# The first three q tiles copied out by ScalarE and multiplied by GpSimd, with one rope moved up and zeros in the first lap

## The reference, cut to what matters

```python
q_hk  = (hidden_q @ Wq.T).reshape(Bv, Sv, H, K)
q_big = jnp.einsum('bshk,hkq->bshq', q_hk, w_kc_q)          # 192 columns a head
q_big = _apply_rope(q_big, sin_q, cos_q)                    # x * cos + rotate_half(x) * sin
q_r   = jnp.einsum('bshq,hqr->bhsr', q_big, W_qr)           # 64 columns a head
scores = jnp.einsum('bhsr,bhlr->bhsl', q_r, k_r)
attn  = jax.nn.softmax(scores, axis=-1)
ctx   = attn @ kv_r, then through w_kc_kv and Wo, added to x with a gate
```

## Time and profile before

| | |
|---|---|
| median of 3 runs | 547.29 us (544.44, 547.29, 547.99) |
| the profiled execution, its time | 546.06 us |
| its span, first to last instruction | 543.9 us |
| hand-over (end of the first mixture to the first scores) | about 206 to 227 us |
| laps | about 227 to 435 us |
| mean granted clock of TensorE | 0.959 of full speed |

### The profile page before, as it was taken

The page is one execution under the profiler, slowest core; times in us unless marked ns, Lnnn a source line. Parts: engine busy times, 40 slices in busy tenths (PEclk is TensorE's granted clock), DMA queues, the critical chain, the costliest instruction groups (busy, mean ns, idle before and its releaser), DMA issues.

```text
span 543.9 us, 9155 instructions
## 1 busy us (share of the span) xinstructions
PE 496.7 (91%) x2775; PEld 382.8 (70%) x2775; DVE 415.2 (76%) x1060; ACT 308.6 (57%) x789; POOL 280.3 (52%) x291
## 2 busy tenths in 40 slices
PE   6886999998997997789999999999998977999996
PEld 3664678876876885557777777777776756778874
DVE  4998599988477658888999999999997874644322
ACT  3744554433644643267877777787777772155541
POOL 0042446765433842658777778786661016436560
PEclk9969799999999999879999999999999996999998
DMA  7659313322422319944727180807004602334426
GB/s 255 206 187 302 135 50 93 87 62 59 145 85 62 88 39 227 180 109 96 150 55 170 36 192 11 193 10 166 1 2 186 290 5 84 107 105 127 127 64 231
DMA packets 40281, 65.02 MB, mean 120 GB/s; under 512 B 4324, under 2 KB 30638, under 8 KB 39985
## 3 DMA queue, kind: packets, MB, share of 16 engines
q1 hardware_dynamic: 37984, 60.31, 39.4%
q0 software_dynamic: 2256, 4.21, 2.4%
HBM read 38.48 MB, written 27.99 MB: 122 GB/s over the span
## 4 chain that ended last, share of the span: by engine, by line
PE 65%; DVE 21%; ACT 4%; issue 3%; DMA 3%; POOL 1%; another core or an unknown queue 1%; SPq 1%; POOLq 0%; DVEq 0%
PE bank L1588 10%; PE bank L802 9%; PE bank L1643 5%; PE bank L1632 5%; PE bank L1662 5%; PE bank L1006 5%; PE bank L837 4%; PE bank L1605 3%; PE bank L1609 3%; PE bank L1622 3%; PE bank L1623 2%; PE bank L1022 2%; DVE xn L359 2%; DVE hid L758 2%; DVE silu L756 2%
## 5 line engine op out<-in xcount | busy, mean ns | idle before, releaser
L1423 POOL TENSOR_TENSOR qr<-qr 128x512 f32<-128x512 f32 x48 | 61.6, 1283 | 15.9 <-DVE qr L2078 15.9
L2078 DVE TENSOR_TENSOR qr<-bank,sinq 64x512 f32<-64x512 f32 x96 | 66.1, 689 | 2.2
L1815 ACT ACTIVATE silu<-bank,negm 128x256 f32<-128x256 f32 x128 | 59.2, 470 | 5.9 <-DVE negm L2092 5.9
L719 POOL TENSOR_TENSOR ffn_w_l<-ffn_raw,ffn_w_h 128x512 fp32r<-128x512 f32 x30 | 39.4, 1315 | 35.3 <-ACT ffn_w_h L731 35.2
L1428 POOL TENSOR_TENSOR hid<-silu,rden 128x256 f32<-128x256 f32 x55 | 33.7, 613 | 36.4 <-DVE rden L2097 36.4
L743 ACT ACTIVATE hid_h<-hid 128x512 fp32r<-128x512 f32 x28 | 17.7, 631 | 55.5 <-DVE hid L758 49.2
L2092 DVE TENSOR_REDUCE negm<-bank 128x2 f32<-128x512 f32 x64 | 44.2, 691 | 6.4 <-PE bank L1623 3.7
L1822 ACT ACTIVATE hid<-silu,rden 128x256 f32<-128x256 f32 x55 | 27.9, 507 | 34.2 <-DVE rden L2097 34.2
L961 POOL DMA_INDIRECT y_rows<-moe_y,route_rows x31 | 30.1, 971 | 30.7 <-issue 16.8
L802 PE MATMUL bank<-xT_h,ffn_w_h 128*128 128x512 f32 x120 | 41.4, 428 | 2.9 <-DVE xT_l L416 2.9
L1828 ACT ACTIVATE probsT<-bank 128x512 f32<-128x512 f32 x64 | 37.9, 592 | 10.1 <-PE bank L1632 9.7
(11 more groups left out here) (255 smaller groups left out, 1395.2 us busy)
## 6 DMA issues: line engine op xcount, KB each, us to landing
xn_slots<-blank SPq DMA_DIRECT2D x8, 2056.0 KB, 12.5
ffn_raw<-in_w_ffn SPq DMA_DIRECT2D x30, 256.0 KB, 2.7
pair_w<-in_pair_w SPq DMA_DIRECT2D x8, 768.0 KB, 5.2
moe_w<-in_w_moe SPq DMA_DIRECT2D x1, 6144.0 KB, 17.9
moe_x<-xn_slots SPq DMA_DIRECT2D x31, 128.5 KB
ffn_raw<-in_w_ffn SPq DMA_DIRECT2D x30, 128.0 KB, 2.4
folds<-att_w_raw SPq DMA_DIRECT2D x6, 640.0 KB, 7.5
att_w_raw<-folds SPq DMA_DIRECT2D x6, 384.0 KB, 12.1
```

Source lines behind the costliest of these rows:

```text
L719: nc.gpsimd.tensor_tensor(wt_l[b][:, 0:GU], raw[b][:, 0:GU], wt_h[b][:, 0:GU], ALU.subtract).then_inc(self.wgl, 1)
L1423: nc.gpsimd.tensor_tensor(qr[n][:, 0, :], qr[n][:, 0, :], qr[n][:, 1, :], ALU.add).then_inc(s_turned, 1)
L1815: last = nc.scalar.activation(ex[u % 2][:, h, :], bank[4 + u % 2][:, h * S:(h + 1) * S], ACT.Exp, bias=negm[:, u % 2, h:h + 1], accum_out= ...
L2078: last = nc.vector.tensor_tensor(by_sin[other, :, :], q2[hs, :, :], sinq[hs, j:j + 1, :].broadcast_to([C, 2, S]), ALU.mult)
```

## The change

It takes the first three q tiles of pair 0 in another way. ScalarE copies each from PSUM into both halves of `qr[n]` (`q_straight`, one instruction, and `q_halves_swapped`, two), and GpSimd multiplies in place by the tables (`products`) before it adds (`turned`). For that the sine table is loaded once more with its halves exchanged (`sin_turned`, two small transfers). The sine part of tile (0,2) stays on VectorE (`first_sin`). The table of the square root is loaded ahead. TensorE's rope of the first half comes before q (0,4) instead of after it. `cos_sin(0, 4)` moves behind `q_low`, and `cos_sin(0, 5)` into slot 0 of the first lap behind `maxima`, with its `turned` in slot 1. In slot 2 of the first lap TensorE multiplies zeros, 4 matmuls before the scores and 8 behind them. The two clearing transfers that stood before the laps stand behind the loop of laps.

```diff
@@ -174,6 +174,7 @@
             pT2 = [lsb(f"probsT{i}", [P, 2, 2, S]) for i in range(4)]
+            sin_turned = pT2[3][:].rearrange("p h k s -> p (h k s)")[:, 0:JT * S].rearrange("p (j s) -> p j s", j=JT)
             cv = [lsb(f"c{i}", [P, 2 * S]) for i in range(2)]
@@ -1358,6 +1359,8 @@
                     sp.dma_start(sinq[:], a["sinq"]).then_inc(s_trig, 16)
+                    for h in range(2):
+                        sp.dma_start(sin_turned[(1 - h) * C:(2 - h) * C], a["sinq"][h * C:(h + 1) * C]).then_inc(s_trig, 16)
                 ffn0.prog_sp(sp, {N0: load_attention})
@@ -1369,8 +1372,6 @@
                 sp.wait_ge(s_zz, 3)
-                for i in range(NPAIR - 2, CLEARS):
-                    clear_slots(i)
                 with sp.Fori(0, (NPAIR - 2) // 2) as ii:
@@ -1382,6 +1383,8 @@
                         clear_slots(ii * 2 + b)
+                for i in range(NPAIR - 2, CLEARS):
+                    clear_slots(i)
                 sp.wait_ge(s_rp, NPAIR * 2 * JT)
@@ -1448,6 +1451,8 @@
                         normalise(before[0], before[2])
+                    if lap.first and n == 1:
+                        turned(0, 2 * JT - 1)
                     tile = lap.cos_tile(n - 1)
@@ -1463,11 +1468,23 @@
                                       2 * N0 - 5: lambda: low_part(1, 1, 0), 2 * N0 - 4: lambda: low_part(1, 1, 1)})
-                turned(0, 0)
-                turned(0, 1)
+                def products(n, part, table):
+                    pool.wait_ge(s_cs, 2 * n + part + 1)
+                    q = qr[n][:, part, :].rearrange("p (b s) -> p b s", b=2)
+                    nc.gpsimd.tensor_tensor(q, q, table[:, n:n + 1, :].broadcast_to([P, 2, S]),
+                                            ALU.mult).then_inc(s_xs, 1)
+                pool.wait_ge(s_trig, 64)
+                for n in range(JT):
+                    products(n, 0, cosq)
+                    if n < JT - 1:
+                        products(n, 1, sin_turned)
+                    pool.wait_ge(s_xs, 4 + min(2 * n + 2, 2 * JT - 1))
+                    turned(0, n)
                 for st in (ffn1_first, ffn1_second):
                     ffn1.low_gateup(pool, st)
-                for n in range(2, 2 * JT):
+                for n in range(JT, 2 * JT - 1):
                     turned(0, n)
@@ -1663,10 +1680,20 @@
                     last.then_inc(s_y, 1)
+                def fill(count, bk):
+                    for _ in range(count):
+                        nc.tensor.matmul(bank[bk][:], zero[:, 0:P], zero[:], start=True, stop=True)
                 def slot(n, lap):
                     unit, rope, half = lap.unit(n, 0), lap.rope(n), lap.half(n)
+                    idle = lap.first and n == TURNED
+                    if idle:
+                        fill(4, 2)
                     if unit:
                         scores(*unit)
+                    if idle:
+                        fill(8, 2)
                     unit = lap.unit(n, TURNED)
@@ -1696,18 +1723,13 @@
                     q_step(i, i, n)
+                pe.wait_ge(s_cs, 2)
                 n_att[1].pe_transpose(pe)
                 n_att[1].pe_whole(pe)
                 q_step(0, 0, 3)
+                rope_step(0, 0, 1, 0)
                 q_step(0, 0, 4)
-                rope_step(0, 0, 1, 0)
                 q_step(0, 0, 5)
-                pe.wait_ge(s_cs, 10)
-
-                def fill(count, bk):
-
-                    for _ in range(count):
-                        nc.tensor.matmul(bank[bk][:], zero[:, 0:P], zero[:], start=True, stop=True)
                 run_laps(slot, pe, {9: lambda: fill(6, 1), 10: lambda: fill(2, 1), 11: lambda: n_ffn1[0].pe_transpose(pe)})
@@ -1875,6 +1897,18 @@
                         high_f(0, 0)
+                def q_straight(n):
+                    act.wait_ge(s_q, n + 1)
+                    nc.scalar.activation(qr[n][:, 0, :], bank[FIRST_BANKS[0, n]][:], ACT.Copy).then_inc(s_cs, 1)
+                def q_halves_swapped(n):
+                    for h in range(2):
+                        hs, other = slice(h * C, (h + 1) * C), slice((1 - h) * C, (2 - h) * C)
+                        last = nc.scalar.activation(qr[n][other, 1, :], bank[FIRST_BANKS[0, n]][hs, :], ACT.Copy)
+                    last.then_inc(s_cs, 1)
                 def second_rows():
@@ -1885,7 +1919,8 @@
                                     2 * N0 - 6: lambda: first_high_parts(1)},
-                              {0: lambda: comb_act(route[0][0], act), N0 + 2: second_rows})
+                              {0: lambda: comb_act(route[0][0], act), N0 + 2: second_rows,
+                               2 * N0 - 2: lambda: q_straight(0)})
                 def split_first_tile():
@@ -1894,12 +1929,18 @@
                 act.sem_inc(s_c, 1)
+                def table(func, at):
+                    nc.scalar.activation(table_out[:, at:at + 1], tg[:, 0:1], func)
+                q_halves_swapped(0)
+                table(ACT.Sqrt, 1)
+                q_straight(1)
+                q_halves_swapped(1)
+                q_straight(2)
                 n_att[1].act_root(act)
                 n_att[1].act_high(act)
                 split_first_tile()
                 q_high(0, 0, 0)
-                def table(func, at):
-                    nc.scalar.activation(table_out[:, at:at + 1], tg[:, 0:1], func)
                 def second_rows_copy(hf):
@@ -2061,18 +2102,25 @@
                     dve.wait_ge(route[0][1].rowc, 2)
-                def first_cos_sin():
-                    dve.wait_ge(s_trig, 32)
-                    cos_sin(0, 0)
+                def first_sin():
+                    dve.wait_ge(s_trig, 64)
+                    dve.wait_ge(s_cs, 2 * JT - 1)
+                    sines(0, JT - 1)
                 def cos_sin(i, n):
                     if not (isinstance(i, int) and i == 0):
                         dve.wait_ge(s_rp, i * (2 * JT) + JT * (n // JT) - JT)
                     dve.wait_ge(s_q, i * 6 + (n + 1 + 2 * (n >= JT and isinstance(i, int) and i == 0)))
                     q2 = bank[bank_of(i, n)][:].rearrange("p (b s) -> p b s", b=2)
-                    j = n % JT
-                    by_cos, by_sin = [qr[n][:, w, :].rearrange("p (b s) -> p b s", b=2) for w in range(2)]
-                    nc.vector.tensor_tensor(by_cos, q2, cosq[:, j:j + 1, :].broadcast_to([P, 2, S]),
+                    by_cos = qr[n][:, 0, :].rearrange("p (b s) -> p b s", b=2)
+                    nc.vector.tensor_tensor(by_cos, q2, cosq[:, n % JT:n % JT + 1, :].broadcast_to([P, 2, S]),
                                             ALU.mult).then_inc(s_cs, 1)
+                    sines(i, n)
+                def sines(i, n):
+                    q2 = bank[bank_of(i, n)][:].rearrange("p (b s) -> p b s", b=2)
+                    j, by_sin = n % JT, qr[n][:, 1, :].rearrange("p (b s) -> p b s", b=2)
                     for h in range(2):
@@ -2140,6 +2188,8 @@
                         normalise(before[0], before[2], heads)
+                    if lap.first and n == 0:
+                        cos_sin(0, 2 * JT - 1)
                     if m is not None:
@@ -2152,19 +2202,17 @@
                                     N0 + 5: lambda: n_att[0].apply(seq),
-                                    2 * N0 - 5: lambda: n_att[0].low(dve)}, topk_round, first_cos_sin)
+                                    2 * N0 - 5: lambda: n_att[0].low(dve)}, topk_round)
                 dve.sem_inc(s_xa, 1)
                 dve.wait_ge(ffn0.acc, 2)
                 n_att[1].stats(seq)
                 n_att[1].scale(dve, seq)
-                cos_sin(0, 1)
+                first_sin()
                 n_att[1].low(dve)
-                cos_sin(0, 2)
                 cos_sin(0, 3)
+                q_low(0, 0, 0)
                 cos_sin(0, 4)
-                q_low(0, 0, 0)
-                cos_sin(0, 5)
                 def first_stats():
```

## The result

The median of the changed kernel is 550.14 us (10 runs, 547.78 to 553.61), that of the kernel before on the same chip 547.01 us. The ratio is 1.0068, its 95% interval 1.0043 to 1.0092: 2.4 to 5.0 us slower, 3.7 in the middle; the two medians are 3.1 us apart. Forecast were 547.5 and no measurable change; 550.14 lies inside the range given, 543.5 to 550.5, by 0.4 us. The profiled execution took 549.71 us with a span of 547.9, 3.65 and 4.0 above the one of before.

What follows compares the result with a forecast made beforehand. The chain up to TensorE's last wait before the closed laps was taken to bound, the rest fixed: +1.5 - 0.65 = +0.85 us gives 546.9 from the profile or 548.1 from the median; middle 547.5, range 543.5 to 550.5.

Steps and rivals of the forecast that it cites:

- The sum sooner: VectorE's sum of the second half, freed of tile (0,0)'s products, starts at 207.3 instead of 208.23, 0.9 us sooner.
- The root behind copies: ScalarE's square root queues behind the q copies and runs at 211.1 instead of 211.62, leaving 0.5 of 0.9 us.
- GpSimd under the norm: GpSimd's products hold up VectorE's small norm steps; norm 1.75 us later instead of 0.5 sooner.
- Rival 1: No or small stall of the norm by GpSimd: -2.85 to -1.2 us, 544.4 to 546.1 us; chance 0.22.
- Sines only: Between `xn` and `xT_l` VectorE does two instructions, not three: 0.7 us sooner; q (0,3) starts at 218.7.
- Rope before q (0,4): On TensorE, q (0,3) at low clock (2.8 us), rope mostly at full (1.9): rope ends at 223.4, bounds 222.0 to 225.1.
- Rival 2: Low clock covers q (0,3) and all of rope, zeros regain nothing: +3.2 us, 549.3 to 550.5 us; chance 0.2.
- The order in VectorE's queue: Three `cos_sin` instead of two between `q_low` and the first reciprocal: 7.25 us, reciprocal at 233.35, 1.5 later.
- Zeros in slot 2: TensorE's zeros in the first lap cost nothing and may keep the clock up for the second rope: 0.65 us back.
- The transfers: Clearings moved behind the loop are covered by SyncE's 46.6 us wait, 9 us to spare; sine loads cost nothing.
- rival 4: The clearing transfers at the end collide with the last block's weights: +1 to +8 us; chance 0.03.
- One to one behind it: Any shift of TensorE's last wait before the closed laps passes unchanged through the rest of the kernel.

Runs made afterwards that it cites:

- a1: The changed kernel without GpSimd's three products of tiles (0,1) and (0,2); ratio to the kernel before 1.0023.
- c1: The changed kernel with products of (0,1), (0,2) held until `xn` is written, root before third copy, old orders, 8 zero matmuls behind the transposes; ratio 0.9987.
- d3: c1 with GpSimd's products no longer held until the norm is done; ratio to the kernel before 1.0027.
- b0: The kernel before, unchanged, measured and profiled again; ratio 1.0005.
- a3: The changed kernel without the 12 zero matmuls in slot 2 of the first lap; ratio to the kernel before 1.0049.
- a2: The changed kernel with zero matmuls in TensorE's hand-over waits, 10 ahead of the second half's transposes and 8 behind; ratio to the kernel before 1.0029.
- d2: c1 with the change's order of rope, `cos_sin(0, 4)` and `cos_sin(0, 5)`; ratio to the kernel before 1.0005.
- e2: The kernel before with a pure delay, 8 zero matmuls on TensorE in the last lap but one; ratio 1.0043.
- e3: The kernel before with a pure delay, 24 zero matmuls on TensorE in the last lap but one; ratio 1.0120.
- e1: The changed kernel, unchanged, a second time beside the kernel before; ratio 1.0045.
- d1: The kernel before with only the two small loads of the exchanged sine table, read by nobody; ratio 1.0005.

## Why the prediction was wrong

**The sum sooner**: right. 207.33 in the frame of before (208.19 - 0.86), forecast 207.3.

**The root behind copies**: right. It starts at 211.07, forecast 211.1; four copies from PSUM stand ahead of it, at 0.60 and 1.20 us as costed. The copy of tile (0,0) delayed `act_high` by nothing.

**GpSimd under the norm**: right in mechanism and size. `xn` starts at 214.58 and ends at 215.96, forecast 214.6 and 216.0. a1, c1 and d3 show that the products are the cause. The Trainium skill (SBUF — State Buffer, "Who interferes with whom") has whoever issues first hold the shared pair of ports for the whole instruction, and the other blocked until then; the ends of the steps 0.02 to 0.03 us behind GpSimd's agree. Rival 1 is out. In a1, where the norm is nearly free, the clock fell all the same, for 3.3 us, though the rival expected no fall behind so short a wait (2.08 us there).

**Sines only**: right, q (0,3) starts at 218.76, forecast 218.7.

**Rope before q (0,4)**: the term that failed. "I expect q (0,3) at the lower level (2.8) and rope mostly at the upper (1.9): rope ends at 223.4." q (0,3) took 2.86, but rope 2.86 too, its first half at the lower level, and it ended at 224.5. The prediction had both rows of the fall and took the shorter one, 3.3 us, since it stood at the same place in the program. That was the length in one execution: b0 has 6.7 us at this place in the kernel before. In the change the fall lasted 6.7, near the 6.8 of the second row. Rival 2, with a chance of 0.2, asked for a start of q (0,3) less than 1 us into the fall, and it came 2.0 us into it (217.6 to 219.62); so rope ran half at the low level and ended at 224.5, between the forecast's 223.4 and the rival's 225.1. In a3's profile, with the fall 1.7 us sooner, the forecast's rope held. a2 shows that the level is the cause, and that it is worth 2.1 us over q (0,3) and rope, of which the forecast had 1.4 in q (0,3).

**The order in VectorE's queue**: right. The first reciprocal stands 7.25 us behind `q_low`'s end (228.01 to 235.26), as forecast; at 234.40 it is 1.05 late, the delay of rope. d2 puts the order alone at +2.1.

**Zeros in slot 2**: right. 0.66 come back, forecast 0.65, and rival 2's clause that they regain nothing after a long fall was wrong: by slot 2 that fall is over, and a3 shows that they keep the clock from falling again. **The transfers**: right, rival 4 is out.

**The sum**: +0.85 was forecast at the last wait, +1.75 measured. The 0.9 more is rope's clock. Passed on one to one it gives 548.8 from the median of before in that comparison (547.01 + 1.75), and measured were 550.14. The 2.6 us between 547.5 and 550.14 are thus 0.9 of rope's clock, 0.4 of the base (the forecast added its 0.85 to 546.65, halfway between the profiled execution and the median, and not to a median), and 1.4 that the hand-over doesn't explain. That 550.14 lies in rival 2's band of 549.3 to 550.5 is luck: the rival wanted 3.2 us in the hand-over, and there were 1.75.

**"One to one behind it"**: it holds for the laps, and e2 and e3 fit it for the rest, within wide intervals. In e1 the time of the change was +2.5 [1.0, 4.0], which fits 1.75 too; the first comparison alone, +3.7 [2.4, 5.0], doesn't. Open remains a surplus in the reworked versions. Their times lie 0.7 to 3.1 us above their hand-overs, most of all in c1, where 3.8 us of hand-over showed as 0.7, while b0, d1, e2 and e3, where the hand-over has the instructions of before, lie -0.2 to +1.1 above hand-over and delay. The profiles put it behind the laps. Ahead of the last down matmuls both groups take the same (206.8 and 207.0 us in the mean), and the laps are fixed; from the laps' end to the last instruction the twelve with a reworked hand-over take 110.8 to 117.1 us, 113.8 in the mean, the five with the old one 111.2 to 114.8, 112.4 in the mean. Of these five, before, b0 and d1 have 111.2 to 111.8, and the two with nothing but a delay 113.3 (e2) and 114.8 (e3). So a longer tail goes with delayed laps too, and it is not a mark of the rework alone; one profile each can't say more. The expectation for b0 put 300 us or more between its last wait and the end, if the tail only scatters; it has 298.4, before has 299.1 and the change 300.5. In the tail the chain goes through single transfers that vary from execution to execution, as the read-back of `y_rows`: 6.55 us before, 7.30 after. I found no instruction that the edits could have moved there, and the cause is not settled.

## What to carry to other kernels

In this kernel work moved to GpSimd was free where VectorE had no chain of small dependent steps on SBUF. Each such step beside a running queue can cost the rest of a GpSimd instruction (1.28 us here; three of four steps paid), so hold that queue until the chain is through. Where TensorE waits just ahead of critical matmuls, cost all of them at the low clock as one bound, or fill the wait: one profile's length of the fall is not the kernel's. And putting a wait's producer sooner is worth nothing when the reader's queue then idles in front of it and carries the same work behind it.

## What the runs showed of the hardware

Not every VectorE instruction is held up by GpSimd. In the changed kernel `bn_stats`, `bn_aggr` and the reciprocal (0.18) ran at their usual length beside 128 x 512 products. So did those that read PSUM and one SBUF tile, as the prediction expected: the sum (0.65 each), and in c1 the sines (1.39 for two) and `xT_l` (1.29 for two). `var<-mv`, a scalar operation on SBUF, is another case. It took 0.21 for 0.17 and ended at 211.57, 0.02 behind the GpSimd instruction that ended at 211.55, and likewise in a2 and d3 (0.03 and 0.02 behind). It was held up like the steps of `refine`, only by an instruction that was nearly done. `hid_l<-hid,hid_h`, 128 x 512 with two SBUF inputs, took 0.99 for 0.69 beside the first product.

TensorE's clock can stay at the low level well beyond the waits ahead of it. In the change the waits were 2.56 and 2.09 us around 1.2 us of transposes, and the low level then lasted 6.7 us, through 4.6 us of matmuls; it was the same in its second profile. In the kernel before the waits were 0.77 and 2.68 us and the low level lasted 3.3, but 6.7 in its second profile (b0) behind the same waits, through 5.9 us of matmuls. Ten and eight matmuls of zeros in the two waits of the change, 4.6 us of TensorE, kept it from falling (a2). Zeros only behind the transposes, in d3, did not keep it up: it fell 0.3 us after their start, they took 3.55 us for what takes 2.1 in a2, and q (0,3) behind them had the full clock.
